# Distance-kernel attention: the off-diagonal blocks of the fourth pair in front of the batch's first value pieces

## The reference

```python
x = L0_attn_a_q                                  # (16, 512, 128)
x = x + attn_a(layernorm(x))                     # the stage with the change
x = x + ffn(layernorm(x)); x = x + ssm(layernorm(x)); x = x + ffn(layernorm(x))

def attn_a(q):
    qh, kh, vh = heads(q @ Wq), heads(q @ Wk), heads(q @ Wv)
    dist = maximum(q_norm - 2.0 * einsum('bhsd,bhtd->bhst', qh, kh) + k_norm.T, 0.0)
    scores = exp(-gamma * SCALE * dist)
    scores = where(triu(ones(S, S), k=1), scores, 0.0)   # only later keys t > s
    return einsum('bhst,bhtd->bhsd', scores, vh) @ Wo
```

## Time and profile before

| | us |
|---|---|
| median of 3 timed runs | 2059.43 (2057.34 to 2061.35) |
| profiled execution, its own time | 2051.54 |
| its span | 2049.6 |
| TensorE busy in the span | 1837.8 (90%) |
| VectorE busy | 1476.5 (72%) |
| ScalarE busy | 1493.7 (73%) |
| attention stage, up to the last r_ot copy | 477.0 |

### The profile page before, as it was taken

How to read it: one execution, slowest core, us unless ns; L and a number is a source line. 1 busy time by engine, 2 the same in 40 slices (tenths; PEclk the granted TensorE clock), 3 DMA queues, 4 the chain that set the end, 5 groups by cost and what they waited for, 6 DMA issues and landing times. The chain is left out here.

```text
span 2049.6 us, 67117 instructions
## 1 busy us (share of the span) xinstructions
PE 1837.8 (90%) x27305; PEld 1283.0 (63%) x27305; DVE 1476.5 (72%) x3582; ACT 1493.7 (73%) x4246; POOL 509.0 (25%) x605
## 2 busy tenths in 40 slices
PE   3888888887899999999979985879999999997998
PEld 1444444443577777677767863537777777775886
DVE  6899999996476788877865654636767767786454
ACT  2999999993788877787745549868888888774554
POOL 2000000000334444344431101014444344343110
PEclk9999999998999999999999997989999999999999
DMA  6655545530000000000011000000000000001101
GB/s 194 150 137 137 135 120 135 134 91 1 12 23 13 23 20 17 18 18 23 13 29 27 2 1 1 1 12 18 19 23 13 23 18 18 23 13 32 45 28 36
DMA packets 77509, 91.87 MB, mean 45 GB/s; under 512 B 11378, under 2 KB 67063, under 8 KB 76647
## 3 DMA queue, kind: packets, MB, share of 16 engines
q1 hardware_dynamic: 75906, 87.15, 16.7%
q10 hardware_dynamic: 1296, 0.44, 0.1%
HBM read 39.67 MB, written 31.10 MB: 35 GB/s over the span
## 5 line engine op out<-in xcount | busy, mean ns | idle before, releaser
L1344 POOL TENSOR_TENSOR f1l_pn<-f1l_p,f1l_rs 128x512 f32<-128x512 f32 (+1 forms) x256 | 208.5, 835 | 312.2 <-DVE f1l_rs L1126 312.2
L1344 POOL TENSOR_TENSOR f2l_pn<-f2l_p,f2l_rs 128x512 f32<-128x512 f32 (+1 forms) x256 | 207.4, 831 | 301.4 <-DVE f2l_rs L1126 301.4
L1039 ACT ACTIVATE f1l_p<-f1l_sm,f1l_nb 128x192 f32<-128x192 f32 x512 | 211.5, 433 | 55.6 <-DVE f1l_nb L1119 55.6
L1039 ACT ACTIVATE f2l_p<-f2l_sm,f2l_nb 128x192 f32<-128x192 f32 x512 | 211.5, 433 | 45.3 <-DVE f2l_nb L1119 45.3
L370 PE MATMUL r_acc<-r_pr,r_vp 128*32 128x128 f32 (+2 forms) x3584 | 204.6, 343 | 28.0 <-ACT r_ot L459 22.6
L480 ACT ACTIVATE r_pr<-r_far 128x1536 f32<-128x1536 f32 x128 | 192.8, 1506 | 21.4 <-PE r_far L356 21.2
L569 DVE SCALAR_TENSOR_TENSOR r_pr<-r_pr,k_lo,r_cap 128x512 f32<-128x512 f32 x256 | 180.1, 746 | 18.6 <-ACT r_pr L480 18.5
L577 DVE TENSOR_SCALAR r_pr<-r_pr,k_hi,k_lo 128x768 f32<-128x768 f32 x256 | 162.2, 677 | 9.6 <-ACT r_pr L480 9.6
L480 ACT ACTIVATE r_pr<-r_near 128x1024 f32<-128x1024 f32 x128 | 139.7, 1091 | 1.0 <-PE r_near L346 1.0
L870 PE MATMUL f2l_pj<-f2l_xt,k_wqkv 128*128 128x512 f32 x244 | 133.0, 627 | 2.2 <-ACT f2l_qt L1019 1.4
L870 PE MATMUL f1l_pj<-f1l_xt,k_wqkv 128*128 128x512 f32 x244 | 133.0, 627 | 2.2 <-ACT f1l_qt L1019 1.4
(11 more groups left out here) (426 smaller groups left out, 4836.7 us busy)
## 6 DMA issues: line engine op xcount, KB each, us to landing
rbf_rows<-r_part SPq DMA_DIRECT2D x112, 128.0 KB, 1.9
r_qs<-rbf_rows SPq DMA_DIRECT2D x60, 192.0 KB
r_ks<-rbf_rows SPq DMA_DIRECT2D x60, 192.0 KB
f1l_vs<-f1l_vv SPq DMA_DIRECT2D x64, 128.0 KB, 2.4
f2l_vs<-f2l_vv SPq DMA_DIRECT2D x64, 128.0 KB, 2.3
rbf_rows<-r_part SPq DMA_DIRECT2D x16, 384.0 KB, 2.5
rbf_rows<-r_part SPq DMA_DIRECT2D x16, 256.0 KB, 2.7
out<-k_x SPq DMA_DIRECT2D x16, 256.0 KB, 2.3
```

What stands on the lines that cost most here:

```text
L1039: ins = nc.scalar.activation(p[:, u % 2, k, :], sm[:, u % 2, k // 2, k % 2 * PW:(k % 2 + 1) * PW], ACT.Exp, bias=nb[:, u % 2, k:k + 1], ac ...
L1344: ins = nc.gpsimd.tensor_tensor(pn[:, u % 2, at:at + HU * w].rearrange("p (k c) -> p k c", k=HU), p[:, u % 2, :, cols], r.broadcast_to([P, ...
```

## The change

In pair w = 3 of every batch `others` is called ahead of `later_values(b, w, 0)`; in the other seven pairs the order stays. As `later_values(b, 3, 0)` and `later_values(b, 3, 1)` are pieces 0 and 1 of q = 0, the two now stand next to each other, behind the blocks off the diagonal.

```diff
         OUT_AT = 4
         NORM_AT = 4
+        FRESH_AT = 3
...
                 for w in range(PAIRS):
                     diagonal(b, b % 2, w)
-                    later_values(b, w, 0)
-                    others(b, b % 2, w)
+                    if w == FRESH_AT:
+                        others(b, b % 2, w)
+                        later_values(b, w, 0)
+                    else:
+                        later_values(b, w, 0)
+                        others(b, b % 2, w)
                     later_values(b, w, 1)
```

## The result

The changed kernel takes 2034.06 us (median of 4 runs, 2031.35 to 2037.64) beside 2058.39 us of the kernel before in the same session: a ratio of 0.9882, with a 95% interval of 0.9867 to 0.9896. The forecast was 2032, in a range of 2024 to 2046. The profiled execution took 2032.38 us for 2051.54 before.

What follows compares the result with a forecast made beforehand. VectorE was taken as nearly the bound (25.22 of 25.95 us a batch). 15.4 + 6.0 - 0.46 = 21.0 gives 2030.6 from the profiled 2051.54, or 2033.0 from the timed median with 5.4 more; forecast 2032, range 2024 to 2046.

Steps and rivals of the forecast that it cites:

- (a): At w = 3, off-diagonal (far) blocks end 0.14 us before value piece 0; ScalarE's 0.56 us wait goes.
- (b): Chain from accumulator copy to next value projection, full clock: 0.43 us shorter per batch, 6.0 us over 14; ScalarE's wait 0.8.
- (c): TensorE's 1.52 us gap at w = 3, cut to 0.95 empty, no longer halves its clock; gains 15.4 us.
- (d): Batch 0, without evacuation to wait for: value pieces wait for far blocks, a loss of 0.46 us.
- (e): Batch 15, no further projection: gain 0; last value pieces at another clock phase, within 1.3 us either way, taken as 0.
- the first (the clock keeps falling): TensorE's clock keeps falling behind the remaining gap: 2043.5 or 2051 us, or 2036 to 2046 if partly; chance 0.19.
- The third, far blocks that delay the value pieces: Late far blocks delay the value pieces in 15 batches, costing 6.9 us, all falls kept: 2066; slower, chance 0.06.
- That VectorE takes the gain back: No change: VectorE or a wait behind w = 3 takes back all; 2051.5 or 2059.4 us, chance 0.05.

Runs made afterwards that it cites:

- The filling alone: Kernel before, old order, with two unused 128x128 matmuls added behind the diagonal of w = 3 in batches 0 to 14; 2039.50 us, ratio 0.9902.
- the version that kept the gap: Changed kernel, but the blocks off the diagonal of w = 3 also wait for the accumulator copy r_ot; 2061.24 us, ratio 1.0013.
- the control: The changed kernel run once more, unaltered, in the session of the experiments; 2034.69 us, ratio 0.9881.

## Why the prediction was right

*(a) The far blocks in the gap*: as worked out. 0.05 us behind their release for 0.06, the margin ahead of the value pieces not used up, ScalarE's 0.56 us gone.

*(b) What is late next*: the right chain, with one term missing. The period at full clock is 25.38 us for a forecast of 25.52, so the gain is 0.57 a batch and not 0.43. The 0.14 lies in the value pieces. Ahead of and behind the far blocks they took 0.79 + 0.78 us from start to next start; side by side they take 161.57 - 160.14 = 1.43. I had moved the blocks and kept the durations of their neighbours. That the change from these float32 matmuls to the bf16 ones and back costs the 0.14 is a likely reading, but it wasn't measured by itself. ScalarE's wait for the projection came out at 0.52 for 0.8. The 0.8 was a slip: the prediction's own times, the exponential's end at 164.15 and r_vp at 164.69, give 0.54. VectorE's idle time of 0.3 a batch was put at 25.52 - 25.22 and is 0.23.

*(c) The clock*: the largest term, 15.4 us, and right in mechanism and size. The filling alone shortens the same 14 batches by 15.2 us in the profiles, and gives 19.8 us against the median before. I had assumed that most timed executions before had more falls than the profiled one. No trace of them shows it; it fits that the version that kept the gap had falls in all 14 batches and a total of 2061, and that the runs of the kernel before lie around 2059. The step was too absolute, though. "I take it that it no longer does" is refuted: behind the 0.95 us gap the clock still fell once in the profiled run and twice in the control, at 1.6 us each, and three times in each of two later runs. The rule of the Trainium skill that I set against my step ("TensorE: Matmul & The Clock Gate", section "A second HAM failure mode: psum-queue depth-cycling": micro-idles between groups of matmuls are enough to make the clock swing) is so borne out in kind: two falls in the control behind a gap of this size. In weight it isn't, 1 to 3 of 14 for 10 to 14.

*(d) Batch 0*: the right sign, the size off by two, 1.06 us for 0.46. Of the difference, 0.1 is a slip in the sum: 55.75 + 1.44 + 0.78 is 57.97, not 57.86. The rest comes of my having the clock return during the value pieces. In the changed kernel both ran at half clock, 55.73 to 58.44, as their time shows, 2.71 us to the next start for 1.43 in batch 4.

*(e) The end*: batch 15 gained nothing of its own, as said. The last stretch was 1.67 us shorter, and the whole of it is the last value pieces at the other clock, 2.38 us for 4.05. TensorE's row in the changed kernel, then in the kernel before:

```profile
452.14 2.38 PE L371 MATMUL r_acc<-r_pr,r_vp 128*32 128x384 f32 x56 [0.49 <-DVE r_pr L582]
```

```profile
472.89 4.05 PE L370 MATMUL r_acc<-r_pr,r_vp 128*32 128x384 f32 x56 [2.06 <-DVE r_pr L577]
```

I had put 0 for it, with 1.3 either way, so it lies outside my bounds. The rest of the kernel was 3.2 us longer, for which I had put 0.

For the profiled pair the terms add up so: 21.0 of the sum, + 2.0 for the 0.14 us in 14 batches (b), - 1.6 for the fall of batch 1 (c), - 0.6 (d), + 1.7 (e), - 3.2 for the stages behind, 19.3 in all; 19.2 were measured. That the misses nearly cancel is luck; the two large terms, the clock's and the overlap's, are not.

The rivals: of the first (the clock keeps falling) one batch in 14 is true. Its total, 2043.5 or 2051, wasn't reached. The third, far blocks that delay the value pieces, is true in batch 0 alone, where there is no evacuation to hide them. That VectorE takes the gain back wasn't so, and the run without the statistics shows why: less work on VectorE leaves the period at 25.38, as the chain from r_ot to the projection is what is left.

## What to carry to other kernels

A gap on TensorE costs more than its length where the clock gives way behind it: here the 3 us of matmuls behind an idle 1.5 us ran at half speed in 10 to 14 of 14 batches, and 0.4 us of work in it, needed or not, took most of that away. So look at the granted clock behind each recurring gap before pricing a reordering, and put into the gap the work that some engine waits for next. An engine busy for 99% of a window need not be its bound; take work from it, or find whose wait ends last.

## What was not expected

Whether a gap brings a fall seems to feed back on itself. In the kernel before four batches of 25.95 to 26.13 us escaped, and from batch 6 on every one fell, at distances that settle from 27.53 to 27.31 us; the version without the overlap settled at the same 27.31 from batch 1 on. The versions whose batches are 25.4 or 25.1 long had one fall or two in a row and then none for several batches. Why the distance settles at this value was not tested.
